# Placing the block sums of a graph network layer by node, with the placing matrix as the weight

## What is computed

```python
def _gine_layer(x, src, dst, w, eps, We, be, W1, b1, gamma, beta, W2, b2):
    m = relu(x[src] + w @ We + be)                 # one message per edge
    agg = segment_sum(m, dst, num_segments=1250)   # summed by destination node
    h = ((1.0 + eps) * x + agg) @ W1 + b1
    h = relu(batchnorm(h, gamma, beta))
    return relu(h @ W2 + b2)
# out = layernorm(x + four layers), all in fp32
```

## Time and profile before

| | |
|---|---|
| median of three runs | 1289.77 us (1289.42 to 1290.07) |
| the profiled execution | 1291.98 us, its span 1290.2 us |
| granted TensorE clock, mean | 0.965 |
| TensorE / VectorE / ScalarE / GpSimd busy | 94% / 80% / 43% / 61% |
| edge phases by the trace | layer 0: 99 to 367 us; layers 1 to 3: 404 to 659, 699 to 955, 1000 to 1248 us |

### The profile page before, as it was taken

One profiled execution on the slowest core, in us unless ns is written; L12 is line 12 of the kernel. 1 busy time (PEld: TensorE's weight loads), 2 busy tenths in 40 slices (PEclk: granted clock), 3 DMA queues, 4 the chain that ended last, 5 costly groups with the idle time before them and its releaser, 6 DMA issues.

```text
span 1290.2 us, 26518 instructions
## 1 busy us (share of the span) xinstructions
PE 1206.8 (94%) x7483; PEld 769.3 (60%) x7483; DVE 1035.1 (80%) x2134; ACT 553.4 (43%) x1159; POOL 783.0 (61%) x831
## 2 busy tenths in 40 slices
PE   2878999999999999999998999999998999999997
PEld 2874566666655566656655566666644566666653
DVE  7988878888866978877776978887767888788768
ACT  1923444444374444434364443434345434443333
POOL 0055677677606777777706777777714777777720
PEclk9558999999999999999998999999989999999999
DMA  3167677667736777777746777777746777777753
GB/s 113 56 189 213 193 207 217 198 203 217 223 104 209 217 217 217 217 217 217 239 132 198 217 216 217 217 217 218 239 127 189 216 217 216 217 217 217 221 179 113
DMA packets 92577, 254.22 MB, mean 197 GB/s; under 512 B 19902, under 2 KB 23114, under 8 KB 92428
## 3 DMA queue, kind: packets, MB, share of 16 engines
q0 software_dynamic: 65600, 215.01, 57.1%
q1 hardware_dynamic: 25804, 36.42, 8.7%
q10 hardware_dynamic: 1024, 1.05, 0.3%
HBM read 239.24 MB, written 12.97 MB: 195 GB/s over the span
## 4 chain that ended last, share of the span: by engine, by line
POOL 42%; PE 29%; issue 15%; DVE 11%; DMA 2%; ACT 1%; ACTq 0%; POOLq 0%; DVEq 0%
POOL rows L827 42%; PE y_ps L2106 10%; PE y_ps L1985 6%; PE pair_ps L1932 4%; DVE rows L1543 3%; DVE rows L1429 2%; PE h_ps L2063 1%; PE y_ps L2117 1%; DMA rows<-node_table,src_fast 1%; PE h_ps L1858 1%; DVE src_onehot L1360 1%; PE uT_ps L2016 1%; DMA node_table<-rows 1%; PE pair_ps L2049 1%; PE uT_ps L2023 1%
## 5 line engine op out<-in xcount | busy, mean ns | idle before, releaser
L827 POOL DMA_INDIRECT rows<-node_table,src_fast x820 | 780.4, 952 | 452.8 <-issue 248.3
L1543 DVE SCALAR_TENSOR_TENSOR rows<-We_ps,negw_fast,rows 128x512 f32<-128x512 f32 x820 | 565.4, 742 | 85.4 <-DMA rows<-node_table,src_fast 84.5
L1985 PE MATMUL y_ps<-table_parts,src_onehot 128*128 128x512 f32 x1664 | 430.9, 410 | 21.8 <-DMA src_onehot<-near_ws 8.5
L1985 PEld LDWEIGHTS y_ps<-table_parts,src_onehot 128*128 128x128 f32 x1664 | 292.6, 191 | 191.8 <-issue 94.3
L1003 ACT ACTIVATE rows<-y_ps 128x512 f32<-128x512 f32 x416 | 248.7, 598 | 217.6 <-PE y_ps L1985 210.8
L1932 PE MATMUL pair_ps<-rows,onehot 128*32 128x512 f32 x2504 | 306.7, 602 | 13.7 <-DVE rows L1543 13.5
L1360 DVE TENSOR_TENSOR src_onehot<-y_ps,src_bc 126x256 fp32r<-126x256 f32 x376 | 149.6, 414 | 60.9 <-PE y_ps L1985 60.4
L1932 PEld LDWEIGHTS pair_ps<-rows,onehot 128*32 128x32 f32 x2504 | 67.9, 109 | 150.5 <-issue 111.8
L2063 PEld LDWEIGHTS h_ps<-uT,W_sb 128*128 128x128 f32 x1152 | 133.8, 192 | 6.0 <-issue 3.3
L2063 PE MATMUL h_ps<-uT,W_sb 128*128 128x128 f32 x1152 | 134.7, 275 | 2.9 <-issue 2.9
L2106 PE MATMUL y_ps<-rows,hT 128*128 128x512 f32 x288 | 124.5, 593 | 0.0
(11 more groups left out here) (251 smaller groups left out, 793.9 us busy)
## 6 DMA issues: line engine op xcount, KB each, us to landing
late_rows<-node_table SPq DMA_DIRECT2D x1536, 2.0 KB
rows<-node_table,src_fast POOLq DMA_INDIRECT x820
b_bc<-node_table ACTq DMA_DIRECT2D x512, 2.0 KB
node_table<-rows SPq DMA_DIRECT2D x29, 256.0 KB, 3.7
src_onehot<-near_ws SPq DMA_DIRECT2D x416, 2.0 KB
x_now<-x_pad SPq DMA_DIRECT2D x10, 512.0 KB, 7.6
W_sb<-W SPq DMA_DIRECT2D x4, 1024.0 KB, 5.5
rows<-W SPq DMA_DIRECT2D x16, 256.0 KB
```

Source lines behind the costliest of these rows:

```text
L827: nc.gpsimd.indirect_dma_start(rows[:, slot, :], None, table[:, :], bass.IndirectOffsetOnAxis(src_fast[:, t:t + 1], 0)).then_inc(landed[q] ...
L1543: last = nc.vector.scalar_tensor_tensor(rows[:, slot, :], We_ps[:, :], negw_fast[:, t:t + 1], row, ALU.mult, ALU.max)
L1985: last = nc.tensor.matmul(y_ps[k % 2][:, :], src_onehot[:, 2 * (k % ONEHOTS) + b, :], table_parts[:, part, 2 * pair_of(k) + b, :], start=( ...
```

## The change

Blocks 0 to 7 of each layer (`BY_NODE` = 8) are placed the other way round. `place_block`, behind quad 1, uses 32 columns of the placing matrix at a time as the weight and moves 512 features: six matmuls (five for block 0), whose result `node_sums` stands by node in the PSUM bank that `uT_ps` uses. VectorE adds it to `u` (`add_sums`, behind the messages of quad 3), and `turn_block`, behind quad 3 on TensorE and ahead of the gathered tiles, transposes the whole `u` into the same bank. ScalarE's order is the same, but `finish_block` now follows `turn_block`. Blocks 8 and 9 are handled as before, except that in the last step the product for block 8 is moved from behind quad 1 to behind quad 2, and VectorE's `keep_w` likewise in layer 0.

```diff
+    BY_NODE = BLOCKS - 2
...
+        node_sums = turned_uT
...
             def scale_u(n, i):
-                if n:
-                    act.wait_ge(u_turned, n)
+                if i == BLOCKS - 1:
+                    act.wait_ge(u_turned, n // BLOCKS * (BLOCKS - BY_NODE) + i - BY_NODE)
+                elif n:
+                    act.wait_ge(block_summed, n + 1)
...
+            def add_sums(n, l, i):
+                dve.wait_ge(u_ready, n + 1)
+                dve.wait_ge(block_placed, BY_NODE * l + i + 1)
+                nc.vector.tensor_tensor(u[:, :], node_sums, u[:, :], ALU.add).then_inc(u_whole, 1)
...
-                        if q == (3 if i < BLOCKS - 1 else 1) and l == 0:
+                        if q == (3 if i < BLOCKS - 1 else 2) and l == 0:
                             keep_w(i).then_inc(w_sum_ready, 1)
...
+                        if q == 3 and 0 < i <= BY_NODE:
+                            add_sums(n - 1, l, i - 1)
...
                     sum_quad(q, l, i)
+                    if q == 3 and 0 < i and not final:
+                        turn_block(n - 1, l, i - 1)
...
-                        if q == (0 if final else 1):
+                        if final and q == 0:
                             open_block(n - 1, l, i - 1, True)
                             add_first_pair(n - 1, l, i - 1)
-                        if q == 1:
+                        if final and q == 1:
                             close_block(n - 1, i - 1)
-                        if q == (1 if final else 3):
+                        if not final and q == 1:
+                            place_block(n - 1, l, i - 1)
+                        if q == (2 if final else 3):
                             product_h(n - 1, l, i - 1)
...
+            def place_block(n, l, i):
+                pe.wait_ge(uT_copied, n + 1)
+                pe.wait_ge(place_ready, n + 1)
+                pe.wait_ge(pair_copied[0], n + 2)
+                pe.wait_ge(pair_copied[1], n + 2)
+                if i:
+                    pe.wait_ge(carry_copied, (BLOCKS - 1) * l + i + 1)
+                nodes = [slice(g * WIN, (g + 1) * WIN) for g in range(P // WIN)]
+                for g in range(PLACED // WIN):
+                    nc.tensor.matmul(node_sums[nodes[g], :], place0(i)[:, nodes[g]], pair_sb[:, 0, :],
+                                     start=True, stop=g == 1 or g == 0 and not i)
+                nc.tensor.matmul(node_sums[nodes[3], :], place1(i, WIN, 2 * WIN), pair_sb[:, 1, :], start=True, stop=True)
+                if i:
+                    nc.tensor.matmul(node_sums[nodes[0], :], place1(i - 1, HALF, PLACED), carry[:, :],
+                                     start=False, stop=True)
+                nc.tensor.matmul(node_sums[nodes[2], :], place1(i, 0, WIN), pair_sb[:, 1, :],
+                                 start=False, stop=True).then_inc(block_placed, 1)
...
+            def turn_block(n, l, i):
+                pe.wait_ge(u_whole, BY_NODE * l + i + 1)
+                for c in range(C):
+                    last = nc.tensor.matmul(uT_ps[:, c, :], u[:, c * P:(c + 1) * P], ident[:, :],
+                                            start=(c == 0), stop=True, is_transpose=True, skip_group_check=True)
+                last.then_inc(block_summed, 1)
```

More of the change, by code:

```diff
@@ L477, in gnn_layers @@
         u_turned = sem("u_turned")
+        block_placed = sem("block_placed")
+        u_whole = sem("u_whole")
         u_ready = sem("u_ready")
```

## The result

| | before | changed |
|---|---|---|
| median, 12 runs each, taken side by side | 1291.27 us | 1297.43 us |
| ratio (95% interval) | | 1.0042 (1.0026 to 1.0058) |
| profiled execution, its span | 1291.98, 1290.2 us | 1299.81, 1298.0 us |
| layer 0, first gather to first matmul of dense | 99.71 to 366.76: 267.05 us | 102.86 to 377.78: 274.92 us |
| from dense to dense, layers 1, 2, 3 | 292.66, 295.75, 293.45 | 293.46, 292.27, 291.96 |

A forecast was written before the change was run, and what follows sets the result against it. POOL's fetches were taken to bound layers 1 to 3, TensorE and VectorE layer 0. Layer 0's terms, 1.5 + 5.5 + 1.5 - 0.7 = +7.8 us, on 1289.77 gave 1297.6 us; range 1289 to 1303.5.

The forecast's parts named there:

- The bound: Layers 1 to 3 go at POOL's pace, layer 0 at TensorE's and VectorE's; 51.3 us of POOL's work per two steps.
- The placing: TensorE, each step: six matmuls in two rounds, 1.85 us, plus 0.49 for transposes, against 3.21 before; 0.87 us saved.
- the seam: TensorE, change of tiling mode between matmuls: two fewer changes in each step, each hiding 0.1 us at most.
- The weight copies: Layer 0: `place_w` waits about 1 us a step for ScalarE's copies; gathers begin 0.23 to 0.49 us later.
- ScalarE's row: ScalarE behind the transposes: 2.2 us of copies before the first activation, against 1.23; 0.98 us charged a step.
- By step: Layer 0: step 1 +1.5, even steps +1.4 each, odd steps 0.45 to 0.5 each, last step -0.7 us.
- the later layers: Layers 1 to 3: POOL's pace stays, so 0 us each, with bounds -0.5 and +1.8 each.
- (a): Whole kernel faster: `place_w`'s wait and the late activations are hidden, 5 us less, 1284.7 us; chance 0.08.
- (b): Whole kernel unchanged: the tiles make up the 0.98 us; about 1291 us; chance 0.17.
- (c): Whole kernel slower by more: late weight rows hold gathers, later layers end 1.0 to 1.8 us later; 1302 us; chance 0.12.
- (d): TensorE: the six matmuls don't overlap, 3.6 us; 9 us per later layer, 14 in layer 0; some 1331 us; chance 0.03.

The follow-up runs named there:

- a2: Changed kernel with the copies of carry and pair 0 moved ahead of `finish_block` on ScalarE; ratio to before 0.9995, layer 0 268.82 us.
- a1: Changed kernel with layer 0's weight copies ahead of the two row loads on ScalarE; ratio to before 0.9965, layer 0 263.08 us.
- a3: Changed kernel with both the weight copies ahead of the row loads and two copies ahead of `finish_block`; ratio to before 0.9955, layer 0 259.22 us.
- b2: Kernel before with only `close_block` moved behind quad 3, same matmuls, no addition; ratio to before 1.0141, layer 0 279.63 us.
- a5: Changed kernel with `add_sums` adding one column of 512; ratio to before 1.0042, layer 0 275.36 us.
- b1: Kernel before with the weight copies ahead of the row loads; ratio to before 1.0007, layer 0 265.45 us.
- b3: Kernel before with the one-hot for quads 4 to 7 made twice in steps 1 to 8; ratio to before 1.0019, layer 0 270.54 us.
- b4: Kernel before with weight copies ahead of row loads and, in the last step, block 8's product behind quad 2; ratio to before 0.9979, layer 0 264.71 us.
- a4: Changed kernel with the product for block 8 and `keep_w` back behind quad 1 in the last step; ratio to before 1.0077, layer 0 273.81 us.

## Why the prediction was right, point by point

**The bound.** Layers 1 to 3 go at POOL's pace: from the 13th fetch of a layer to its last takes 240.1 us in both kernels in each of them (407.26 to 647.36 before, 418.15 to 658.22 after). a2 takes about 1 us a step from TensorE there and their lengths stay (294.0, 293.0, 292.5). Right.

**The placing.** Forecast 1.85 us, measured 1.7, and the transposes 0.41 rather than 0.49. In layer 1, where no `place_w` hides it:

```profile
570.04 1.92 PE L1947 MATMUL pair_ps<-rows,onehot 128*32 128x512 f32 x16
571.78 0.61 PE L2058 MATMUL uT_ps<-pair_sb,place 128*32 128x512 f32 x3
...
572.63 0.59 PE L2062 MATMUL uT_ps<-carry,place 128*32 128x512 f32 x1
572.64 0.62 PE L1947 MATMUL pair_ps<-rows,onehot 128*32 128x512 f32 x1
...
575.32 0.66 PE L2071 MATMUL uT_ps<-ident,u 128*128 128x128 f32 x4
575.73 2.08 PE L2004 MATMUL y_ps<-table_parts,src_onehot 128*128 128x512 f32 x8
578.85 3.10 PE L2004 MATMUL y_ps<-table_parts,src_onehot 128*128 128x512 f32 x12 [1.04 <-ACT rows L1010]
```

From the placing to the gathers 3.95 us, against 565.79 - 560.72 = 5.07 before: 1.12 saved, 0.87 forecast; and then 1.04 of waiting. The two quads ahead of the placing take 1.74 us (570.04 to 571.78) instead of 1.85, since no matmul of 128x128 follows them: the seam that was put at 0.1 us at most is 0.11.

**The weight copies.** Forecast about 1 us of waiting in each step; measured 1.05 to 1.42 in steps 1 to 8 and 0.24 in step 9. The gathers begin 0.19 us later in step 4 (220.57 to 228.22 against 213.77 to 221.23), 0.39 forecast; the difference is the shorter transposes (0.08) and the seam (0.11).

**ScalarE's row.** Forecast 0.98 us; from the first gather to the product it is 228.22 to 235.19, 6.97 us, against 5.83: 1.14. The row is 2.37 us long, 2.2 forecast.

**By step**, added to layer 0: step 1 +1.4 (forecast 1.5); even steps +1.4, 1.3, 1.3, 1.6 (1.4); odd steps +0.37, 0.43, 0.30 (0.45 to 0.5); last stretch -0.63 (-0.7). With +0.35 ahead of step 1's placing, which was not forecast, it is 7.87, forecast 7.8. a1, a2, a3 and b2 show that two waits on ScalarE are the cause, a5 that VectorE's addition is not more than what the odd steps show.

**Where it was lucky, and where not.** The median came to 1297.43 us for 1297.6, but the change itself was 5.4 us for 7.8: the forecast started from 1289.77 us, the median of three runs, and the twelve runs beside the changed kernel have 1291.27. The profiled span grew by 7.8 us as forecast, but not by layer 0 alone: +3.15 before the first gather, in code that the change doesn't touch, +7.87 in layer 0, -4.2 in layers 1 to 3, +0.9 at the end. The first is spread between executions: the first gather is at 99.6 to 102.9 us in the eleven profiles, at 102.9 in one with the old placing too (b1). For the later layers the forecast was 0 with bounds of -0.5 and +1.8 each, and -4.2 in three is outside. Most of it looks like spread too. With the fetches at the same pace, 3.2 of the 4.2 us lie between the last fetch and dense: 12.06, 14.71 and 13.14 us before, 13.02, 11.99 and 11.67 after. The longest of before and one of 17.06 us in a3 have a mean granted clock of 0.77 and 0.70, all others of before, changed and a3 1.00 (columns as under b2, before and then a3):

```profile
940.46:955.17 14.71, 11.70 (x65) 7.39 (x63) 9.53 (x31) 2.06 (x7) 0.95 (x1) 0.77 0.26 84
...
640.30:657.36 17.06, 14.24 (x72) 10.24 (x67) 9.69 (x32) 2.59 (x9) 0.94 (x1) 0.70 0.24 71
```

So the hit of the profiled span, 7.8 for 7.8, is luck in its parts outside layer 0; that of layer 0 is not. Why the twelve runs of each kernel give 5.4 us and not 7.8 (the interval reaches 7.5) stays open. A gain in the later layers would explain it and is not shown: the means from dense to dense are 293.2 to 294.0 us in the four profiles with the old placing in its place (before, b1, b3, b4), 292.6 to 293.4 in the changed kernel, a1, a2, a4 and a5, but 294.6 in a3.

**The rivals.** (a) was kept from happening by ScalarE's order: with that mended (a3) the kernel is 0.45% faster than before, where (a) had 5 us, 0.4%; the two orders of b4 have a part in that. (b) is refuted by the 1.14 us, (c) by the unchanged later layers, (d) by the 1.7 us of a placing.

## What to carry to other kernels

Before work is taken off the busiest engine, follow its neighbours' program order: who must finish before the next instruction behind the shortened piece can start, and which instructions of another engine are queued behind the event that is moved. Here moving four transposes behind quad 3 put four copies ahead of an activation on which a ring of two banks turned; a few lines of order on ScalarE were worth 12 us in steps 2 to 9 of layer 0 and turned a loss of 0.4% into a gain of 0.45%. And a wait that costs nothing because something longer covers it (b1) has to be written down with its cover.

## What the runs showed of the hardware

- TensorE's granted clock falls for a few us in the midst of work: two quads then take 3.2 to 3.5 us instead of 1.92. It did so in step 1 of layer 0 in before, changed, a5, b2 and b3 and not in the other six profiles, and once each later in that layer (a5 in step 8, b2 in step 4), so a single profile's layer carries 1.6 to 1.7 us for each. The code of step 1 alone doesn't decide it: a4 has that of the changed kernel and takes 27.46 us there, not 29.04. None of the four profiles with the weight copies first has the drop and five of the other seven do, so that order may keep it away; one profile of each doesn't settle it. The busy time of the changed kernel around such a stretch, and then in two quads of it (length, busy of PE, PEld, DVE, ACT, POOL, then the granted clock, DMA share, GB/s). 0.81 and 0.57 are mixes of the two levels, 1.2 and 2.4 GHz, and before the fall TensorE had waited 1.32 us for the weight copies:

```profile
137.50:144.50 7.00, 5.68 (x36) 1.54 (x28) 4.81 (x10) 0.43 (x3) 5.48 (x6) 0.81 0.75 220
141.39:144.55 3.16, 3.16 (x18) 0.56 (x16) 3.02 (x7) 0.00 (x0) 2.55 (x3) 0.57 0.77 217
```

- Matmuls into one window of 32 partitions don't hold those into the others, across lines of code too. The six of a placing use windows 0 and 2 twice; in layer 1 the second turn starts at 572.63, 0.85 us behind the first at 571.78, quad 2's first matmul at 572.64, beside it, and all 14 matmuls of placing and two quads take 575.32 - 571.78 = 3.54 us, where two quads alone take 1.85.
